# Layer 0's remainder tile: a negated copy and an accumulating DMA in place of a VectorE subtraction

## The reference

```python
e = stack([tbl_f[ids[:, f]] for f in range(32)], axis=1)          # 1024 x 32 x 32
def layer(h, W, b):                                               # O = 128, 128, 1
    z = einsum('bhd,bmd,ohm->bod', h, e, W.reshape(O, H, 32))
    return relu(z + b[None, :, None])
z0 = layer(e, W0, b0); h1, direct0 = z0[:, :64], z0[:, 64:]
z1 = layer(h1, W1, b1); h2, direct1 = z1[:, :64], z1[:, 64:]
z2 = layer(h2, W2, b2)
z = sum over d of concat(direct0, direct1, z2)                    # 1024 x 129
y = relu(relu(concat(z, dense_ctx) @ W_top1 + b_top1) @ W_top2 + b_top2) @ W_top3
```

## Time and profile before

| | |
|---|---|
| median of 3 runs | 1181.24 us |
| lowest and highest | 1178.46 and 1185.1 us |
| the profiled execution | 1183.08 us, of which the span of the trace is 1181.2 us |
| TensorE busy | 1126.7 us (95% of the span) |
| VectorE busy | 1082.9 us (92%) |
| GpSimd busy | 514.5 us (44%) |
| ScalarE busy | 460.0 us (39%) |
| TensorE's granted clock | 0.997 of full speed |

### The profile page before, as it was taken

How to read it: one execution, slowest core, us unless ns; L and a number is a source line. 1 busy time by engine, 2 the same in 40 slices (tenths; PEclk the granted TensorE clock), 3 DMA queues, 4 the chain that set the end, 5 groups by cost and what they waited for, 6 DMA issues and landing times.

```text
span 1181.2 us, 10957 instructions
## 1 busy us (share of the span) xinstructions
PE 1126.7 (95%) x3608; PEld 652.1 (55%) x3608; DVE 1082.9 (92%) x604; ACT 460.0 (39%) x383; POOL 514.5 (44%) x270
## 2 busy tenths in 40 slices
PE   0789999999999999999999999999999999999998
PEld 0345555555555555556555555555556555555554
DVE  1599999999999999999999999999999999999973
ACT  0234444433444433344443334444333444443424
POOL 6604444555444455544445554444555444450000
PEclk9999999999999999999999999999999999999999
DMA  7744443454545344454434455443445544333100
GB/s 222 222 138 133 137 152 121 118 139 137 159 137 142 121 126 136 140 157 138 140 118 130 127 148 148 147 138 120 132 127 148 154 141 142 128 120 112 54 0 1
DMA packets 63413, 154.94 MB, mean 131 GB/s; under 512 B 12753, under 2 KB 29394, under 8 KB 63394
## 3 DMA queue, kind: packets, MB, share of 16 engines
q1 hardware_dynamic: 37202, 96.64, 23.2%
q10 hardware_dynamic: 18000, 53.85, 17.3%
q0 software_dynamic: 8192, 4.21, 3.6%
HBM read 95.79 MB, written 8.39 MB: 88 GB/s over the span
## 4 chain that ended last, share of the span: by engine, by line
DVE 36%; issue 23%; ACT 11%; ACTq 11%; PE 9%; DMA 9%; DVEq 1%; SPq 1%
DVE prod L398 13%; DVE prod_lo L444 12%; DVE raw L437 9%; PE z_ps L530 8%; ACTq L726 5%; ACT prod_hi L753 5%; ACTq L727 5%; DMA x_roll<-x_dram 4%; ACT h_roll L716 4%; DMA x_part<-x_dram 4%; ACT direct L720 1%; DVE raw L420 1%; DVE lo L427 1%; PE mlp_ps L530 1%; SPq L349 1%
## 5 line engine op out<-in xcount | busy, mean ns | idle before, releaser
L530 PE MATMUL z_ps<-prod,w_sb 128*128 128x512 f32 x1536 | 696.5, 600 | 48.1 <-issue 28.4
L303 POOL DMA_INDIRECT gathered<-in_table,rows_sb x256 | 509.9, 1992 | 522.1 <-DVE h2x L451 451.5
L530 PEld LDWEIGHTS z_ps<-prod,w_sb 128*128 128x128 f32 x1536 | 288.5, 191 | 367.2 <-issue 335.0
L753 ACT CAST prod_hi<-raw 128x2048 fp32r<-128x2048 f32 x128 | 244.1, 1907 | 424.4 <-DVE raw L437 365.8
L444 DVE TENSOR_TENSOR prod_lo<-raw,prod_hi 128x2048 fp32r<-128x2048 f32 x128 | 292.3, 2284 | 26.5 <-ACT prod_hi L753 26.5
L437 DVE TENSOR_TENSOR raw<-h_roll,x_roll 128x2048 f32<-128x2048 f32 x128 | 292.7, 2287 | 3.3 <-DMA h_roll<-h_roll 0.9
L398 DVE TENSOR_TENSOR prod<-h_roll,x_roll 128x2048 f32<-128x2048 f32 x128 | 292.5, 2285 | 0.0
L530 PE MATMUL z_ps<-prod_hi,w_hi 128*128 128x512 f32 x520 | 214.9, 493 | 3.0 <-DVE prod_lo L444 3.0
L530 PE MATMUL z_ps<-prod_hi,w_lo 128*128 128x512 f32 x520 | 164.2, 395 | 0.0
L530 PE MATMUL z_ps<-prod_lo,w_hi 128*128 128x512 f32 x520 | 164.1, 395 | 0.0
L398 DVE TENSOR_TENSOR prod<-x_base,x_roll 128x2048 f32<-128x2048 f32 x63 | 143.4, 2287 | 15.1 <-DMA x_roll<-x_dram 8.4
(11 more groups left out here) (56 smaller groups left out, 231.9 us busy)
## 6 DMA issues: line engine op xcount, KB each, us to landing
x_roll<-x_dram SPq DMA_DIRECT2D x128, 512.0 KB
x_base<-x_dram SPq DMA_DIRECT2D x32, 512.0 KB
h_roll<-h_roll ACTq DMA_DIRECT2D x32, 448.0 KB, 3.4
h_roll<-h_roll ACTq DMA_DIRECT2D x32, 384.0 KB
h_roll<-h_roll ACTq DMA_DIRECT2D x32, 320.0 KB
x_dram<-gathered SPq DMA_DIRECT2D x64, 128.0 KB
h_roll<-h_roll ACTq DMA_DIRECT2D x32, 192.0 KB
h_roll<-h_roll ACTq DMA_DIRECT2D x33, 128.0 KB
```

Source lines behind the costliest of these rows:

```text
L303: nc.gpsimd.indirect_dma_start(gathered[:, u, g * DIM:(g + 1) * DIM], None, table, bass.IndirectOffsetOnAxis(ap=rows_sb[:, col:col + 1], a ...
L530: return nc.tensor.matmul(*args, **kw)
L753: nc.scalar.copy(prod_hi[:, b % SPLIT_RING, :, :], raw[:, :, :]).then_inc(hi_ready, 1)
```

## The change

`lo16` is no longer made by VectorE. ScalarE writes -raw16, rounded to float32r, into `lo16` right after `hi16`, and GpSimd issues a DMA that adds the float32 `raw16` onto it in SBUF, so that raw16 - round(raw16) stays. `lo16_ready` now rises by 16 when that DMA has landed, and TensorE waits for it and for `hi16_ready`. GpSimd's gather code is rewritten so that these DMAs stand between the gathers.

```diff
+            def make_rows(group):
...
+            def gather(u, made, freed):
...
+            def add_raw16(rounded):
+                pool.wait_ge(ids_loaded, 32)
+                pool.wait_ge(minus16_ready, rounded)
+                nc.gpsimd.dma_start(lo16[:, :], raw16[:, :], accum_op=ALU.add).then_inc(lo16_ready, 16)
+
+            make_rows(0)
+            for u in range(UNROLL):
+                gather(u, 1, 0)
+            for c in range(2):
+                add_raw16(c + 1)
+            with pool.Fori(0, CHUNKS // UNROLL - 1) as group:
+                freed = [settled(pool, group * UNROLL + u + 1) for u in range(UNROLL)]
+                rounded = [settled(pool, group * UNROLL + u + 3) for u in range(UNROLL)]
+                made = settled(pool, group + 2)
+                make_rows(group + 1)
                 for u in range(UNROLL):
...
+                    add_raw16(rounded[u])
+                    gather(u, made, freed[u])
+            for c in range(CHUNKS - 2, CHUNKS):
+                add_raw16(c + 1)
...
-                wait(dve, lo16_ready, c)
+                wait(dve, lo16_ready, 16 * c)
...
-            def split_rest16(c):
-
-                dve.wait_ge(hi16_ready, c + 1)
-                wait(dve, pairs16_used, c)
-                nc.vector.tensor_tensor(lo16[:, :], raw16[:, :], hi16[:, :], ALU.subtract).then_inc(lo16_ready, 1)
...
-                    if b == 0 and not is_last(c):
-                        split_rest16(c + 1)
...
-                pe.wait_ge(lo16_ready, c + 1)
+                pe.wait_ge(hi16_ready, c + 1)
+                pe.wait_ge(lo16_ready, 16 * (c + 1))
...
                 nc.scalar.copy(hi16[:, :], raw16[:, :]).then_inc(hi16_ready, 1)
+                nc.scalar.mul(lo16[:, :], raw16[:, :], -1.0).then_inc(minus16_ready, 1)
```

More of the change, by code:

```diff
@@ L210, in build_tower @@
         hi16_ready = sem("hi16_ready")
+        minus16_ready = sem("minus16_ready")
         lo16_ready = sem("lo16_ready")
@@ L282, in _ @@
             pool.wait_ge(ids_loaded, 32)
-            def gather_group(group):
+            def make_rows(group):
                 cols = UNROLL * GATHERS
-                made = settled(pool, group + 1)
-                freed = [0 if isinstance(group, int) else settled(pool, (group - 1) * UNROLL + u + 1)
-                         for u in range(UNROLL)]
                 for u in range(UNROLL):
@@ L293, in gather_group @@
                                         ALU.add).then_inc(rows_made, 1)
+            def gather(u, made, freed):
                 pool.wait_ge(ids_loaded, 32)
                 pool.wait_ge(rows_made, made)
-                for u in range(UNROLL):
[L299 to L310, removed]
+                wait(pool, h2x_ready, freed)
+                for g in range(GATHERS):
+                    col = u * GATHERS + g
+                    nc.gpsimd.indirect_dma_start(
+                        gathered[:, u, g * DIM:(g + 1) * DIM], None, table,
+                        bass.IndirectOffsetOnAxis(ap=rows_sb[:, col:col + 1], axis=0),
+                    ).then_inc(gather_done[u], 16)
+            def add_raw16(rounded):
[12 more added lines that the diff above has]
+                make_rows(group + 1)
+                for u in range(UNROLL):
+                    add_raw16(rounded[u])
+                    gather(u, made, freed[u])
+            for c in range(CHUNKS - 2, CHUNKS):
+                add_raw16(c + 1)
         @block.sync
@@ L498, in _ @@
             products0(0, 0, 0)
-            split_rest16(0)
             dve.wait_ge(w1_loaded, 48)
```

## The result

The changed kernel takes 1211.18 us (median of 4 runs, 1204.45 to 1216.83) against 1181.93 for the kernel before (4 runs): a ratio of 1.0246, 95% interval 1.0184 to 1.0308. It is slower by 29 us, where I had forecast 9. The direction and the wide range (1182 to 1214) held; the size did not, and the forecast's own range (1189 to 1199) was missed.

What follows compares the result with a forecast made beforehand. VectorE was taken to set the pace, with TensorE about 0.8 us a chunk behind. Saving -9, groups +3 and start +15 gave +9 us, 1192 us; own range 1189 to 1199, 8 in 10 1182 to 1214.

Steps and rivals of the forecast that it cites:

- What bounds the kernel: VectorE with its waits sets the pace, 34.46 us a chunk; TensorE has about 0.8 us of room.
- The saving: Subtraction removed from VectorE: 0.30 us a chunk over 30 chunks, -9 us, bounds -10.2 and -6.
- ScalarE's pass: Added 128x256 pass on ScalarE, about 0.41 us, hides in 1.87 us of idle time.
- The usual chunk: In steady state the new DMA chain to TensorE lands in time and costs nothing.
- L: Time from the start of `raw16` to `lo16` landed; 5.7 us in usual chunks, free up to about 6.9.
- The start: Chunk 0's accumulating DMA queues behind all 32 gathers, delaying layer 1: +15 us, bounds 13.5 and 20.
- a relief at the `h_roll` copies: At the start, later `h_roll` copies meet quiet queues and take 2.8 us less.
- The first chunk of each group: DMA stands behind the row numbers, L = 7.5: +4 us over seven groups, lowered to +3, bounds 0 and +16.
- My price: At TensorE's wait for `lo16`, each microsecond of L above about 6.9 us costs one.
- in every fourth chunk alone: Sign in the changed profile: TensorE idle ahead of the small matmuls only there would show the groups' cost.
- The rival of a slow landing: At TensorE's `layer0_pairs16`, L above 6.9 us makes a wait in every chunk: +36, 1219 us; chance 0.17.
- The range: Range for 8 in 10, 1182 to 1214 us: most of the cancelled case and the slow landing's cheaper half.

Runs made afterwards that it cites:

- e5: Changed kernel without the accumulating DMA: raw16 is never added, waits go to the negated copy, output wrong; 1173.29 us, ratio 0.9910 to the kernel before.
- e4: Changed kernel with a subtraction of the same size back on VectorE at its old place, into a tile nobody reads; 1195.86 us, ratio 1.0115.
- e6: Changed kernel with row numbers made behind a group's first accumulating DMA, and remainders of chunks 0 and 1 by VectorE's subtraction; 1174.42 us, ratio 0.9916.
- e2: Changed kernel with chunk 0's accumulating DMA issued behind the gathers of chunk 2 instead of chunk 3; 1202.66 us, ratio 1.0158.
- e8: Changed kernel with SyncE's load of x_base held until the accumulating DMA of the chunk before has landed; 1190.05 us, ratio 1.0048.
- e7: Changed kernel with 16 unused small matmuls on TensorE ahead of its wait for lo16 in each group's first chunk; 1205.52 us, ratio 1.0179.
- e1: Changed kernel with GpSimd making a group's row numbers behind its first accumulating DMA instead of ahead; 1188.54 us, ratio 1.0060.

## Why the prediction was right and where it failed

**What bounds the kernel:** right. VectorE led with 0.8 us of room behind it; e5 shows the removed work coming out of the time, and e4 shows it going back in.

**The saving:** right in size. I had 0.30 us a chunk and -9 us; e5 measures 0.29. In the changed kernel the 23 usual chunks show 0.44, more than the 0.34 that was removed. e5 and e6, which have no stalls, show 0.29 and 0.30; the rest I take for the engines' catching up behind each stall, which was not tested by itself.

**ScalarE's pass:** right, hidden (e5).

**The usual chunk, L between 4.2 and 7.4, taken as 5.7:** right in the verdict (no wait), off in the parts. The landing, put at 2.2 us behind the end of the issue, is 3.2 - 0.98 = 2.2. The issue itself takes 0.98 us beside VectorE's products, not 1.9; so L is 1.74 + 3.2 = 4.9 us. Here I let the row of the gathers overrule the rule on descriptor generation in the Trainium skill (SBUF — State Buffer, "Who interferes with whom"), and for a DMA that is not indirect the rule was the better guide: 0.98 us beside the products, 0.86 to 1.02 in the first three chunks. The same section has a second half that I did not use: a VectorE instruction with two SBUF inputs contends with a GpSimd instruction that reads SBUF. By that half the row numbers are the instruction in danger, and the trace agrees with it, with 2.30 us in place of 0.48.

**The start, +15 us:** right, 15.4, by the steps given: 54.27 for the first small matmul (I had 55.8 or one less), relu0 at 56.35 (56.5), and a relief at the `h_roll` copies of 1.7 us where I had 2.8 (issued until 62.95, they held VectorE until 67.42: 4.5 us instead of 6.2). relu0 was 17.2 us late, not 17.4, so the term came out as the sum of steps that were each near. e2 and e6 confirm its cause.

**The first chunk of each group, +3 us: this is the step that failed.** In the prediction's terms L was 7.5 us there and measured 9.9, and the clock was put at nothing. The chunk's cost measured 38.53 - 34.02 = 4.5 us in each of six chunks, 27 us, past its bound of 16. I wrote that the row numbers "start at 502.57 and end at 503.05" and took that 0.48 us over into the changed kernel. But the change removes the very instruction beside which they ran; they now fall under the wide product and take 2.2 to 2.4 us (e4). That alone moved the DMA from 3.1 to 4.9 us behind `raw16`, which put it into `x_base`'s load (e8: 5.0 us to land, 2.8 without it), which made TensorE idle for 2.3 to 3.1 us, and with that its clock was halved (e7: some 2 us). My price, one microsecond for each above 6.9, gives 3.0 us for L = 9.9; it held where the clock stayed at 1.00 (e2: L = 10.1, 37.20 - 34.1 = 3.1 us), and the 1.5 us on top of it I put down to the clock. The three do not add up one by one. TensorE asks for `lo16` only 6.0 us after `raw16` and about 0.9 us more are free, so each of e1, e4 and e8 takes away most of the whole: 22.6, 15.3 (after paying for 31 added instructions of 0.33 us) and 21.1 us in the total time. I also counted seven groups; the first falls into the start, and six remain. My text said that TensorE would idle "in every fourth chunk alone", and this sign was right.

**The rival of a slow landing** stayed away as I had put it: in the usual chunks L is 4.9, far from 6.9. Its mechanism was right for one chunk in four.

**The range.** That 1211 us lies inside 1182 to 1214 is in part luck. The upper end came from the cheaper half of the slow landing in every chunk, which did not happen; the loss that filled it was one that I had bounded at 16 us and that came to 27.

## What to carry to other kernels

When an instruction is taken away, look not only at who waited for it but at what ran beside it on other engines: a short instruction between two long ones can be the gap in which another engine's instruction gets through. A small transfer on the critical path should be issued before, not behind, whatever the issuing engine has to do that can wait, and kept apart in time from large loads with slack. An idle stretch on TensorE can cost more than its length, because the clock may fall with it: the six of the changed kernel were 2.7 us long in the mean and cost 4.5 us each.

## What the runs showed of the hardware

- A GpSimd `tensor_tensor` of 128x32 int32 took 0.4 to 0.55 us beside a VectorE instruction of 128x256 (before, e4), and 2.2 to 2.4 us when a 128x2048 `tensor_tensor` began in the 0.2 us ahead of it (after), ending some 0.1 us behind that one. Once, begun under one wide instruction and held through the next, it took 4.9 us (e1, chunk 2). Begun less than 0.1 us before the wide one it took 0.25 us twice (e7) and 2.5 us twice (e6).
- An accumulating DMA from GpSimd, 128 KB within SBUF, float32 added onto float32r: issue 0.86 to 1.02 us, landing 3.2 us after the issue began (median; 2.7 at the least), 4.7 to 5.2 us when a 512 KB load was issued 0.0 to 0.2 us ahead of it (after), 5.7 us at the start beside loads of chunk 1 (e2).
- TensorE's granted clock fell to 0.50 with an idle stretch of 2.39 us and stayed at 1.00 with others of 2.73 and 3.15 us in the same execution (e2). In the changed kernel it fell during or just behind all six stalls of 2.3 to 3.1 us, and in e8 it stayed at 1.00 with all stalls, of up to 1.0 us.
